# Counting stage of a graph kernel: GpSimd folds three partial sums, two products place a group instead of four

## The reference

```python
src_h = h[src] @ W_msg.T + b_msg
emb = edge_embed[jnp.clip(edge_type, 0, NUM_EDGE_TYPES)]
messages = jax.ops.segment_sum(src_h + emb, dst, num_segments=num_nodes)
h_new = _gru_cell(messages, h[:num_nodes], W_ih, W_hh, b_ih, b_hh)
x = _layernorm(x + h_new)
x = _layernorm(x + gnn_layer_1(x, src, dst))   # gathers by src, gates, sums by dst
```

## Time and profile before

| What | Value |
|---|---|
| median of 3 runs | 3452.20 us |
| time of the profiled execution | 3451.43 us |
| its span in the trace | 3449.6 us |
| TensorE (PE) busy, whole span | 2380.8 us, 69% |
| VectorE (DVE) busy | 2628.8 us, 76% |
| ScalarE (ACT) busy | 1804.1 us, 52% |
| GpSimd (POOL) busy | 1620.7 us, 47% |
| granted TensorE clock, mean | 0.77 of full speed |

### The profile page before, as it was taken

One profiled execution on the slowest core, in us unless ns is written; L12 is line 12 of the kernel. 1 busy time (PEld: TensorE's weight loads), 2 busy tenths in 40 slices (PEclk: granted clock), 3 DMA queues, 4 the chain that ended last, 5 costly groups with the idle time before them and its releaser, 6 DMA issues. The chain is left out here.

```text
span 3449.6 us, 69044 instructions
## 1 busy us (share of the span) xinstructions
PE 2380.8 (69%) x15214; PEld 1914.4 (55%) x15214; DVE 2628.8 (76%) x13751; ACT 1804.1 (52%) x3973; POOL 1620.7 (47%) x1687
## 2 busy tenths in 40 slices
PE   1799999999999994555555555555555565555653
PEld 1577777777776543554555544454455555454542
DVE  7777777777774357888888888888888888888888
ACT  2566666666664334545554545445545545455441
POOL 2400000000000003777777777777777777777772
PEclk6899999999999888666666667666666656666665
DMA  6200000000000007555555555655556565665552
GB/s 121 60 0 0 0 0 0 0 0 0 0 0 0 1 25 230 166 163 160 166 158 168 157 168 160 166 163 162 164 158 168 156 170 158 167 161 166 163 160 74
DMA packets 308104, 367.24 MB, mean 106 GB/s; under 512 B 145567, under 2 KB 200799, under 8 KB 308078
## 3 DMA queue, kind: packets, MB, share of 16 engines
q0 software_dynamic: 79088, 215.63, 22.6%
q1 hardware_dynamic: 226778, 150.70, 16.4%
q10 hardware_dynamic: 2212, 0.60, 0.1%
HBM read 348.23 MB, written 17.66 MB: 106 GB/s over the span
## 5 line engine op out<-in xcount | busy, mean ns | idle before, releaser
L1306 POOL DMA_INDIRECT got<-rows,idx x1624 | 1546.2, 952 | 534.7 <-issue 506.7
L1472 PE MATMUL sum_ps<-whot,got 128*128 128x128 f32 x3264 | 692.6, 382 | 655.9 <-DVE whot L1318 570.3
L1472 PEld LDWEIGHTS sum_ps<-whot,got 128*128 128x128 f32 x3264 | 596.6, 274 | 743.8 <-DVE whot L1318 638.5
L835 PE MATMUL span_ps<-x_parts,work 128*126 128x393 bf16 x4028 | 877.6, 331 | 0.0
L807 ACT CAST work<-c_ps 128x318 bf16<-128x318 f32 x1596 | 661.5, 433 | 352.2 <-PE c_ps L863 338.6
L1465 PE MATMUL er_ps<-win,hot_t 128*128 128x128 bf16 x4932 | 528.8, 286 | 242.3 <-ACT hot_t L1416 215.5
L1374 DVE CUSTOM_DVE_ANT_0 pr_s<-got,er_ps 128x128 f32<-128x128 f32 x1624 | 370.0, 283 | 361.9 <-DMA got<-rows,idx 354.4
L1465 PEld LDWEIGHTS er_ps<-win,hot_t 128*128 128x128 bf16 x4932 | 470.4, 134 | 284.6 <-ACT hot_t L1416 244.4
L835 PEld LDWEIGHTS span_ps<-x_parts,work 128*126 128x126 bf16 x4028 | 539.0, 135 | 135.9 <-issue 8.2
L1157 POOL DMA_DIRECT2D dst_row<-sums x1 | 1.2, 1167 | 1146.5 <-DVE sums L1094 1146.5
L739 DVE TENSOR_SCALAR right<-codes_f,now 128x318 bf16<-128x318 f16 x1596 | 490.6, 308 | 0.0
(11 more groups left out here) (236 smaller groups left out, 1779.8 us busy)
## 6 DMA issues: line engine op xcount, KB each, us to landing
work<-dst_row SPq DMA_DIRECT2D x413, 256.0 KB, 3.6
got<-rows,idx POOLq DMA_INDIRECT x1624
win<-parts SPq DMA_DIRECT2D x118, 96.0 KB
idx<-src_tab SPq DMA_DIRECT2D x413, 2.0 KB
parts<-split SPq DMA_DIRECT2D x13, 384.0 KB, 2.6
rows<-nodes SPq DMA_DIRECT2D x13, 256.0 KB, 2.9
rows<-work SPq DMA_DIRECT2D x13, 256.0 KB, 3.2
small_rows<-in_x_dram SPq DMA_DIRECT2D x2, 1547.0 KB
```

Of the source, the lines that this page charges most:

```text
L835: mm = pe.matmul(span_ps[0:ROWS, h, 0:PW], cols_sb[:, h, b, :], x_parts[:, b, 0:PW], start=(b == 0), stop=(b == HI - 1))
L1306: pool.indirect_dma_start(got[:, c, i, :], None, rows, bass.IndirectOffsetOnAxis(ap=idx1[:, c, i:i + 1], axis=0)).then_inc(gathered[c], 16)
L1472: mm = pe.matmul(sum_ps[:, 0:P], got[:, c, i, D:2 * D], whot[:, c, i, :], start=(c == 0 and i == 0), stop=(c == NS - 1 and i == STEP - 1))
```

## The change

After it, `post` on TensorE does one fp32 product (`whole_s`, 126x128, by `place`) and one bf16 product (`kinds_b`, 126x9, by a bf16 copy of the placing matrix, `place_b`). The three parts are added on GpSimd before that: `fold` does two fp32 additions of 126x128 and a cast of 126x9 to bf16 for each group, in a loop of its own that stands ahead of the leftover loop's gathers in GpSimd's queue. VectorE makes `place_b` beside `place`. `post(g-2)` moves from behind tile 5 to behind tile 9 (POST).

```diff
--- before.py
+++ after.py
@@ -598,6 +598,9 @@
             now = sb("now", [P, 2, 3, CG], F32, ph)
             turned_s = sb("turned_s", [P, 2, PW], F32, ph)
             place = sb("place", [P, 2, P], F32, ph)
+            place_b = sb("place_b", [P, 2, P], BF16, ph)
+            whole_s = sb("whole_s", [P, 2, D], F32, ph)
+            kinds_b = sb("kinds_b", [P, 2, NT], BF16, ph)
             c_ps = psum("c_ps", [P, CB, 512], F32, ph)
             span_ps = psum("span_ps", [P, 2, 512], F32, ph)
             out_ps = psum("out_ps", [P, 512], F32, ph)
@@ -625,6 +628,8 @@
             applied = sem("applied")
             s_copied = sem("s_copied")
             place_done = sem("place_done")
+            half_folded = sem("half_folded")
+            folded = sem("folded")
             posted = sem("posted")
             added = sem("added0")
             at_begun = sem("at_begun")
@@ -640,7 +645,7 @@
             drained = sem("drained")
             ft, fr = N // NODES, N % NODES
             PAIRS = CGN // 2
-            POST, BLOCKS = 5, 2
+            POST, BLOCKS = 9, 2
 
             @contextmanager
             def every_left(eng):
@@ -686,6 +691,21 @@
                     pool.memset(nodes[:, ft:NTL, :], 0.0).then_inc(nodes_set, 1)
                     pool.memset(sums[:, 0:NPAD], 0.0).then_inc(zeroed0, 1)
                     pool.memset(counts[:, 0:NPAD], 0.0).then_inc(zeroed0, 1)
+
+                    def fold(g, h):
+
+                        pool.wait_ge(s_copied, g + 3)
+                        pool.wait_ge(posted, g + 1)
+                        pool.tensor_tensor(whole_s[0:ROWS, h, :], turned_s[0:ROWS, h, 2 * D:3 * D],
+                                           turned_s[0:ROWS, h, D:2 * D], ALU.add).then_inc(half_folded, 1)
+                        pool.tensor_copy(kinds_b[0:ROWS, h, :], turned_s[0:ROWS, h, 3 * D:PW]).then_inc(folded, 1)
+                        pool.wait_ge(half_folded, g + 1)
+                        pool.tensor_tensor(whole_s[0:ROWS, h, :], whole_s[0:ROWS, h, :],
+                                           turned_s[0:ROWS, h, 0:D], ALU.add).then_inc(folded, 1)
+
+                    with pool.Fori(0, PAIRS) as k:
+                        for h in range(2):
+                            fold(2 * k + h, h)
                     with every_left(pool) as k:
                         for c in range(NC):
                             pool.wait_ge(idx_in[c], 16 * k + 16)
@@ -711,6 +731,9 @@
 
                     def place_of(g, h):
                         dve.tensor_scalar(place[0:ROWS, h, :], iota_f[0:ROWS, :],
+                                          column_no[0:ROWS, :, :].rearrange("p b g -> p (b g)")[:, bass.ds(g, 1)],
+                                          None, ALU.is_equal).then_inc(place_done, 1)
+                        dve.tensor_scalar(place_b[0:ROWS, h, :], iota_f[0:ROWS, :],
                                           column_no[0:ROWS, :, :].rearrange("p b g -> p (b g)")[:, bass.ds(g, 1)],
                                           None, ALU.is_equal).then_inc(place_done, 1)
 
@@ -842,13 +865,11 @@
                         pe.wait_ge(s_copied, g + 1)
 
                     def post(g, h):
-                        pe.wait_ge(s_copied, g + 3)
-                        pe.wait_ge(place_done, g + 1)
+                        pe.wait_ge(folded, 2 * g + 2)
+                        pe.wait_ge(place_done, 2 * g + 2)
                         pe.wait_ge(added, 2 * g + 2)
-                        for i in range(3):
-                            pe.matmul(out_ps[:, 0:P], turned_s[0:ROWS, h, i * D:(i + 1) * D], place[0:ROWS, h, :],
-                                      start=(i == 0), stop=(i == 2))
-                        pe.matmul(out_ps[0:NT, P:2 * P], turned_s[0:ROWS, h, 3 * D:PW], place[0:ROWS, h, :],
+                        pe.matmul(out_ps[:, 0:P], whole_s[0:ROWS, h, :], place[0:ROWS, h, :], start=True, stop=True)
+                        pe.matmul(out_ps[0:NT, P:2 * P], kinds_b[0:ROWS, h, :], place_b[0:ROWS, h, :],
                                   start=True, stop=True).then_inc(posted, 1)
 
                     def count_pair(k, first):
```

## The result

The changed kernel takes **3431.4 us** (median of 6 runs, 3427.7 to 3432.7), the kernel before 3452.8 (6 runs, 3451.7 to 3456.5): ratio 0.9934, interval 0.9922 to 0.9947. It is faster by 21 us, where 36 were forecast; the time lies in the stated range, near its upper end (which the prediction gives once as 3432 and once as 3434). The profiled execution took 3431.29 us, its span is 3429.5.

What follows compares the result with a forecast made beforehand. The prediction took PE to bound the counting stage. Placing saves 48.8 us and the moved gathers cost 13.2, in sum -35.6 us, for a median of 3416 us, range 3403 to 3432 (also given as reaching 3434).

Steps and rivals of the forecast that it cites:

- What bounded the kernel: Counting stage: PE is busy throughout at full clock, so only less PE work saves time; DVE and ACT have room.
- What PE saves: Placing (`post`) in the counting loop: 1.08 us falls to 0.42, saving 0.66 us a group, -48.8 us over 74 groups.
- change of type: In `post`: 0.07 us of PE time for going from fp32 to bf16 work, kept in the new placing.
- What is added beside it: Counting loop: `place_b` on DVE (0.27 us) and folding on POOL (about 1.05 us) a group, both hidden, cost nothing.
- the margin of 3.2 us: Counting loop: time from POOL seeing the copy to `post` behind tile 9, available for a folding chain of 1.05 us.
- What is moved: Leftover stage: the 28 gathers now stand behind the last fold, delaying the last chunk by +13.2 us (+10 to +20).
- The sum: Whole kernel: -48.8 + 13.2 = -35.6 us, giving a median of 3416 us, range 3403 to 3432.
- The signs: Counting loop and tail: period 12.2 instead of 12.9 us; wrong if PE waits for `folded` or gathers start 8 us late.
- 1: Counting loop: POOL too slow, PE waits each group; needs a chain over 3.2 us; 3500 us with 2.0 us additions; 5%.
- 2: Leftover tail eats the gain: slow loop entry and low clock make it about +25 us, total 3437 us; chance 9%.
- 3: Leftover tail: PE's clock rises, the last chunk costs 3.3 us less, total 3413 us; chance 3%.
- 4: Placing: alternating bf16 and fp32 products cost their own pauses, `post` takes 0.9 us, total 3451 us; chance 3%.

Runs made afterwards that it cites:

- e1_warm: Changed kernel plus one small GpSimd addition (128x8) right after clearing the accumulators, long before the first fold: 3424.4 us, ratio 0.9909 to the kernel before.
- e4_late: Kernel before plus one wait, so GpSimd starts its 28 gathers only after the last copy of turned_s, without folds: 3464.2 us, ratio 1.0030.
- e6_extra3: Changed kernel with each fold's first addition done three more times into idle buffers: 3962 us against 4006 for the kernel before there, ratio 0.988; counting 963.1 us.
- e7_extra6: Changed kernel with each fold's first addition done six more times into idle buffers: 3999 us against 4006 for the kernel before there, ratio 0.997; counting 1002.6 us.

## Why the prediction came out as it did

**What bounded the kernel: right.** PE had no gap in the loop before, and after it has none but the 4.7 us at the first placing; VectorE's and ScalarE's room was real.

**What PE saves: the right mechanism, 0.05 us too much.** The placing takes 0.47 us where 0.42 was put down. The fp32 pair costs 0.31 rather than 0.25 (610.53 - 610.22) and bf16 product and change of type together 0.16 instead of 0.17, so the mis-sized term is the pair: 0.127 us a record was a mean over six of unequal length. Narrow windows on PE show the last record of the six of before and that of the two of now:

```profile
613.26 0.28 PE L849 MATMUL out_ps<-place,turned_s 126*128 126x128 f32 x1
613.47 0.39 PE L851 MATMUL out_ps<-place,turned_s 126*9 126x128 f32 x2
```
```profile
610.33 0.27 PE L871 MATMUL out_ps<-place,whole_s 126*128 126x128 f32 x1
610.53 0.22 PE L872 MATMUL out_ps<-place_b,kinds_b 126*9 126x128 bf16 x1
```

A record that has another of its line behind it takes 0.11 us (610.33 - 610.22), the last one of a line 0.20 (610.53 - 610.33, and 613.47 - 613.26). In the kernel before the next line is fp32 too, so the 0.07 us that the prediction called the change of type isn't one: L849 and L851 each end with such a longer record. 74 x 0.61 = 45.1 us instead of 48.8. e1_warm has 46.5 for the whole counting stretch.

**What is added beside it: the missing term.** The additions take 0.40 to 0.55 us (medians 0.47 and 0.45), the cast 0.18 to 0.25, the chain 1.28 instead of 1.05. All of it was inside the margin of 3.2 us and would have changed nothing. The estimate of 0.28 us plus dispatch for an addition, from the Trainium skill ("GPSIMD Engine Reference", Elementwise — side-by-side cycle accounting), leaves 0.17 to 0.19 us of the medians for all that isn't in its rate. What failed is that each operation on GpSimd was priced as in the steady state. The first addition comes 6.9 us behind its configuration, PE waits 4.7 us for it and loses 3 more at the low clock: 7.9 us that the sum did not have, half of its error. The Trainium skill has this ("GPSIMD Engine Reference", Instruction dispatch: the first call to a freshly loaded kernel pays about 6 us more, with no instruction shown). The trace agrees in size, with 6.9 us here and 6.9 to 7.7 in the other profiled runs where nothing hid it. That it is the loading of code which takes this time is the Trainium skill's account, and no run here shows it. The trace of before held the sign too. The views of its lines L336 (the all-reduce) and L1512 (the last stage) have the configuration instruction, both times under a wait of tens of us:

```profile
L336 POOLq MODIFY_POOL_CONFIG  x2: 1/1/1, 20.7 to 20.8; - x2
L1512 POOLq MODIFY_POOL_CONFIG  x2: 11/11/11, 3393.2 to 3393.2; - x2
```

I had not looked for it. In the changed kernel the last stage's line (L1533) has none, so the fold's configuration served it too. Whether the pause belongs to the first addition as such or to the return from what the all-reduce needed was not tried: in every kernel here the all-reduce comes first.

**What is moved: right.** +13.2 us were put down, +14.5 came, 12.9 of them in e4_late without any fold. The gathers took 35.7 us from the first to the last instead of 34.5, the entry to the loop 1.5 us (1.4 was assumed).

**The sum.** -48.8 + 13.2 = -35.6 became -45.1 + 7.9 + 14.5 = -22.7. That the measured time still lies in the range is luck in part: the range had no allowance for a single late fold, and the 7.9 us fitted into what was kept for a dearer placing and a longer tail, with less than 1 us to spare at 3432. The spans differ by 20.1: counting came out 1.4 us shorter than -45.1 + 7.9, and the stages that the change doesn't touch 4.0 us longer. That is of the size by which these stages differ between kernels in which they are the same: X to D takes 142.7 to 150.2 us in the first six. Their node products run partly at the low clock, and what share differs from trace to trace (stretch, length, busy us by engine, PEclk), in the kernel before, the changed one and e1_warm:

```profile
1136.50:1281.70 145.20, 138.62 (x416) 67.53 (x416) 68.40 (x186) 52.88 (x81) 0.00 (x0) 0.93 0.00 1
```
```profile
1111.00:1253.80 142.80, 135.67 (x416) 66.03 (x416) 68.40 (x186) 52.47 (x81) 0.00 (x0) 0.95 0.00 1
```
```profile
1104.30:1254.50 150.20, 143.71 (x416) 69.26 (x416) 68.39 (x186) 52.95 (x81) 0.00 (x0) 0.90 0.00 0
```

**The signs.** The prediction named as a sign of being wrong that PE waits for `folded` in the loop. It did so once, in the first group, and in none after that. The group's period is 12.41 us instead of 13.02 (median distance of two copies); the difference is the 0.61, where 12.2 and 12.9 had been written down.

**The rivals.** 1 did not happen, and e6_extra3 and e7_extra6 lie on either side of the threshold that it was given. In 2 the tail was 14.5 us, not 25. In 3 the clock stayed low: a leftover tile takes 0.93 us in every kernel. The Trainium skill's rule that sustained work opens the gate ("TensorE: Matmul & The Clock Gate", What's actually happening) would have made this the likely case, and the trace speaks against it here too. 4 did not happen: the bf16 product and what goes with the change of type cost 0.16 us together, 0.17 had been put down; how the 0.16 divides no run shows.

## What to carry to other kernels

Before work is put on an engine that was idle, list what already stood in its queue and would now stand behind it: here 28 gathers that had been free cost a third of the gain, and spreading them one by one between the new work, 28 of them in 28 groups, gave all of it back. With the first addition's pause hidden by the same edit, the gain is 1.4% in total instead of 0.7%. The first addition or multiplication on GpSimd came 6.9 to 7.7 us late in this kernel, once, so it should be done where nobody waits, or at least outside a loop whose waits come first. A fold that takes 1.3 us of an idle engine is free only if its reader comes late enough: moving the reader four tiles down was worth as much as three quarters of the saving.

## What the runs showed that I had not expected

- A configuration instruction on GpSimd's queue ahead of its first addition, and 6.9 to 7.7 us until the addition runs, for 126x128 and for 128x8 alike. Where it runs differed between two forms of the same fold: at 106.0 us in straight code, at 127.6 behind the waits of a loop. It isn't dear by itself: the changed kernel has one ahead of each fold in its loop, and only the first is followed by a pause.
- 28 gathers between the additions cause no second such pause.
- Two fp32 records of 126x128 by 128 columns start 0.11 us apart and the last of a line takes 0.20, so such a product costs 0.22 us inside a row of them and 0.31 at its end.
- Stages that no edit touches differed by up to 7.5 us between profiled runs together with their mean granted clock (0.90 to 0.95).
- A placing that PE had to wait for takes 0.57 us instead of 0.47, beside the wait.
